# First stage of a gated cross-attention layer: x loaded from ScalarE's queue, weights alone in SyncE's and rounded one unit ahead, context and two units of weights loaded ahead of x

## What is computed

```python
x = x + tanh(g_xattn[0]) * xattn(layernorm(x), ctx, ctx, mask, wq, wk, wv, wo)
x = x + tanh(g_ffn[0]) * ffn(layernorm(x), weight, bias, gate_w, in_scale, out_scale)

# xattn: 32 query heads, 8 heads of keys and values, 128 wide, rotary positions
q = rope(heads(layernorm(x) @ wq)); k = rope(heads(ctx @ wk)); v = heads(ctx @ wv)
out = softmax(q @ k.T / sqrt(128) + mask) @ v;  return merge(out) @ wo
```

## Time and profile before

| | us |
|---|---|
| median of 3 runs (1532.45 to 1533.03) | 1532.85 |
| the profiled execution, its own time | 1532.2 |
| its span, first to last instruction | 1530.4 |
| PE busy in the span | 1485.5 (97%) |
| POOL busy | 723.7 (47%) |
| ACT busy | 613.2 (40%) |
| DVE busy | 1032.1 (67%) |
| share of PE in the chain that ended last | 83% |
| first matmul of the second stage starts at | 90.57 |

### The profile page before, as it was taken

How to read it: one execution, slowest core, us unless ns; L and a number is a source line. 1 busy time by engine, 2 the same in 40 slices (tenths; PEclk the granted TensorE clock), 3 DMA queues, 4 the chain that set the end, 5 groups by cost and what they waited for, 6 DMA issues and landing times.

```text
span 1530.4 us, 26067 instructions
## 1 busy us (share of the span) xinstructions
PE 1485.5 (97%) x8720; PEld 1307.6 (85%) x8720; DVE 1032.1 (67%) x2373; ACT 613.2 (40%) x1183; POOL 723.7 (47%) x594
## 2 busy tenths in 40 slices
PE   5989999999999999999999989999999999989998
PEld 5868888888888888888888879999999999977886
DVE  5837888888877888888887784455455555765653
ACT  5732222222222212222222255555567555634442
POOL 6834445654555445554465453333333333335554
PEclk9999999999999999999999999999999999999999
DMA  7830222212221322212221596443997443542311
GB/s 272 287 110 27 71 76 69 69 48 69 75 69 45 85 69 75 69 41 75 69 69 44 166 361 227 132 131 100 369 390 230 134 125 102 185 141 109 110 74 64
DMA packets 95210, 192.56 MB, mean 126 GB/s; under 512 B 9056, under 2 KB 36192, under 8 KB 95008
## 3 DMA queue, kind: packets, MB, share of 16 engines
q1 hardware_dynamic: 88944, 179.74, 36.4%
q10 hardware_dynamic: 6192, 11.86, 2.3%
HBM read 133.90 MB, written 57.67 MB: 125 GB/s over the span
## 4 chain that ended last, share of the span: by engine, by line
PE 83%; DMA 3%; issue 3%; POOL 2%; DVE 1%; SPq 1%; ACT 1%; POOLq 0%; ACTq 0%; DVEq 0%
PE bank L54 19%; PE bank L53 19%; PE bank L52 19%; PE bank L916 7%; PE bank L915 7%; PE bank L914 7%; PE bank L937 5%; DMA w_raw<-in_wo 2%; POOL last_rows L1352 1%; PE bank L950 1%; DVE project L1504 1%; SPq L689 0%; POOL feed L1344 0%; ACT project L1130 0%; DMA signs_scratch<-rows 0%
## 5 line engine op out<-in xcount | busy, mean ns | idle before, releaser
L52 PE MATMUL bank<-x_hi,w_hi 128*128 128x512 f32 x1024 | 399.6, 390 | 3.9 <-PEq L67 3.9
L54 PE MATMUL bank<-x_hi,w_lo 128*128 128x512 f32 x1024 | 400.6, 391 | 0.0
L53 PE MATMUL bank<-x_lo,w_hi 128*128 128x512 f32 x1024 | 400.0, 391 | 0.0
L1504 DVE TENSOR_TENSOR project<-bank,project 64x256 fp32r<-64x256 f32 x512 | 216.1, 422 | 196.0 <-ACT project L1130 190.6
L1357 POOL TENSOR_TENSOR w_lo<-w_raw,w_hi 128x512 fp32r<-128x512 f32 x128 | 166.4, 1301 | 283.8 <-ACT w_hi L1122 283.8
L1291 POOL TENSOR_TENSOR q_lo<-rot,q_hi 128x512 fp32r<-128x512 f32 x128 | 165.0, 1295 | 188.4 <-ACT q_hi L1061 188.2
L1130 ACT CAST project<-bank 64x256 fp32r<-64x256 f32 x512 | 187.6, 366 | 159.2 <-PE bank L54 150.4
L915 PE MATMUL bank<-project,project 128*128 128x256 f32 x832 | 236.3, 284 | 0.0
L914 PE MATMUL bank<-project,project 128*128 128x256 f32 x832 | 236.2, 284 | 0.0
L916 PE MATMUL bank<-project,project 128*128 128x256 f32 x832 | 235.9, 284 | 0.0
L52 PEld LDWEIGHTS bank<-x_hi,w_hi 128*128 128x128 f32 x1024 | 192.7, 188 | 45.4 <-issue 4.1
(11 more groups left out here) (143 smaller groups left out, 2683.8 us busy)
## 6 DMA issues: line engine op xcount, KB each, us to landing
w_raw<-in_wo SPq DMA_DIRECT2D x128, 256.0 KB, 3.0
project<-probs_scratch SPq DMA_DIRECT2D x52, 512.0 KB, 8.8
w_raw<-in_wq SPq DMA_DIRECT2D x32, 512.0 KB, 5.2
probs_scratch<-pt_hi SPq DMA_DIRECT2D x64, 256.0 KB, 2.6
probs_scratch<-pt_lo SPq DMA_DIRECT2D x64, 256.0 KB, 3.2
x_in<-in_x SPq DMA_DIRECT2D x16, 512.0 KB, 5.0
last_rows<-in_x SPq DMA_DIRECT2D x8, 1024.0 KB, 6.1
x_scratch<-last_rows SPq DMA_DIRECT2D x8, 1024.0 KB, 6.0
```

The costliest lines, as they stand in the source:

```text
L52: pe.matmul(out, hi, rhs_hi, start=first, stop=False, **kw)
L53: pe.matmul(out, hi, rhs_lo, start=False, stop=False, **kw)
L54: return pe.matmul(out, lo, rhs_hi, start=False, stop=last, **kw)
L1504: done = nc.vector.tensor_tensor(vw_lo[i][at], vw_ps[hp % VW_BANKS][b * SK:(b + 1) * SK, h, :], vw_hi[i][at].bitcast(F32), ALU.subtract)
```

## The change

Five edits, all in `prepare`:

1. On SP, both halves of the context and units 0 and 1 are issued first, then blocks 0 to 2 of x. From then on SP loads only weights, and it takes over the stores of keys and values, at fixed places between the loads (`KEYS_AT`, `VALUES_AT`), with the waits at the end of the stage.
2. On ACT, `load_x(n + 3)` stands in iteration n right behind `normalise(n)`, whose result it waits for.
3. On ACT, `split_unit` runs one unit ahead: unit 0 between the two halves of the context, and unit n + 1 at the head of iteration n, ahead of `normalise(n)`.
4. On POOL, `reciprocal_deviation(0)` no longer stands ahead of the loop; iteration n makes `w_lo` of unit n and then `reciprocal_deviation(n - 1)`.
5. On DVE, the low part of the context comes ahead of the statistics of block 0.

```diff
@@ SyncE
+    KEYS_AT, VALUES_AT = 6, HKV + 6
-            def load_x(i):
-                wait(sp, xn_ready, i - XB + 1)
-                sp.dma_start(x_in[:, i % XB], a["x"][i * P:(i + 1) * P, :]).then_inc(x_in_sem[i % XB], 16)
+            def store_keys(gp):
+                sp.wait_ge(k_roped, gp + 1)
+                for c in range(2):
+                    sp.dma_start(scratch["keys"][c, gp * P:(gp + 1) * P, :], k_rot[:, 2 * c, :]).then_inc(k_stored, 16)
+
+            def store_values(g):
+                sp.wait_ge(v_lo_ready, g + 1)
+                for c, part in enumerate((v_hi, v_lo)):
+                    sp.dma_start(scratch["values"][c, g], part[:, g % 2].bitcast(F32)).then_inc(v_stored[g % 2], 16)
 
             for h in range(2):
                 src = a["ctx_t"].rearrange("(k p) t -> p k t", p=P)[:, half(h)]
                 sp.dma_start(ctx_raw[:, half(h)], src).then_inc(ctx_in[h], 16)
-                if h == 0:
-                    load_unit(0)
-                    load_x(0)
-            load_unit(1)
-            load_x(1)
-            load_x(2)
+                load_unit(h)
+            for i in range(XB):
+                sp.dma_start(x_in[:, i], a["x"][i * P:(i + 1) * P, :]).then_inc(x_in_sem[i], 16)
             for n in range(2, UNITS):
                 load_unit(n)
-                if n + 1 < NLN:
-                    load_x(n + 1)
+                if n >= KEYS_AT and n % 2 == 0 and (n - KEYS_AT) // 2 < GP:
+                    store_keys((n - KEYS_AT) // 2)
+                if n >= VALUES_AT:
+                    store_values(n - VALUES_AT)
+            for g in range(UNITS - VALUES_AT, HKV):
+                store_values(g)
...
@@ ScalarE
+            def load_x(i):
+                act.wait_ge(xn_ready, i - XB + 1)
+                act.dma_start(x_in[:, i % XB], a["x"][i * P:(i + 1) * P, :]).then_inc(x_in_sem[i % XB], 16)
...
             for h in range(2):
                 act.wait_ge(ctx_in[h], 16)
                 nc.scalar.copy(ctx_hi[:, half(h)], ctx_raw[:, half(h)]).then_inc(ctx_hi_ready, 1)
+                if h == 0:
+                    split_unit(0)
             for n in range(NU + 2):
-                split_unit(n)
+                if n + 1 < UNITS:
+                    split_unit(n + 1)
                 if n < NLN:
                     normalise(n)
+                if n + XB < NLN:
+                    load_x(n + XB)
                 if HKV <= n - 1 < NU:
                     value_high(n - 1 - HKV)
                 if n >= 2:
                     turned(n - 2)
-
-                if 0 <= n - 2 < HKV and (n - 2) % 2 == 1:
-                    store_keys((n - 2) // 2)
-                if n - 2 >= HKV:
-                    store_values(n - 2 - HKV)
...
@@ GpSimd
-            reciprocal_deviation(0)
             for n in range(UNITS):
                 for h in range(2):
                     pool.wait_ge(w_hi_ready, 2 * n + h + 1)
 
                     nc.gpsimd.tensor_tensor(w_lo[:, n % 2, half(h)], raw(n)[:, half(h)], w_hi[:, n % 2, half(h)].bitcast(F32),
                                             ALU.subtract).then_inc(w_lo_ready, 1)
-                if n + 1 < NLN:
-                    reciprocal_deviation(n + 1)
+                if 0 <= n - 1 < NLN:
+                    reciprocal_deviation(n - 1)
@@ VectorE
-            statistics(0)
             for h in range(2):
                 dve.wait_ge(ctx_hi_ready, h + 1)
                 ...
+            statistics(0)
```

More of the change, by code:

```diff
@@ L149, in _ @@
                 sp.dma_start(ctx_raw[:, half(h)], src).then_inc(ctx_in[h], 16)
-                if h == 0:
-                    load_unit(0)
-                    load_x(0)
-            load_unit(1)
-            load_x(1)
-            load_x(2)
+                load_unit(h)
+            for i in range(XB):
+                sp.dma_start(x_in[:, i], a["x"][i * P:(i + 1) * P, :]).then_inc(x_in_sem[i], 16)
             for n in range(2, UNITS):
                 load_unit(n)
-                if n + 1 < NLN:
-                    load_x(n + 1)
+                if n >= KEYS_AT and n % 2 == 0 and (n - KEYS_AT) // 2 < GP:
[4 more added lines that the diff above has]
+                store_values(g)
+            sp.wait_ge(k_stored, 32 * GP)
+            for i in range(2):
+                sp.wait_ge(v_stored[i], 32 * HKV // 2)
         @block.tensor
@@ L215, in turned @@
                 last.then_inc(x_hi_ready, 1)
[L217 to L225, removed]
             act.dma_start(ident[:], a["ident"]).then_inc(ident_in, 16)
@@ L240, in _ @@
                     turned(n - 2)
-                if 0 <= n - 2 < HKV and (n - 2) % 2 == 1:
-                    store_keys((n - 2) // 2)
-                if n - 2 >= HKV:
-                    store_values(n - 2 - HKV)
-            act.wait_ge(k_stored, 32 * GP)
-            for i in range(2):
-                act.wait_ge(v_stored[i], 32 * HKV // 2)
         @block.gpsimd
```

## The result

| | before | changed |
|---|---|---|
| median of 6 runs, us | 1532.94 (1531.31 to 1535.17) | 1568.83 (1566.58 to 1570.67) |
| ratio | 1 | 1.0236, 95% interval 1.0224 to 1.0247 |
| span of the profiled execution | 1530.4 | 1565.6 |
| first matmul of the second stage | 90.57 | 126.33 |
| block 0 normalised at | 12.82 | 14.79 |

The change makes the kernel 2.4% slower, and all of it lies ahead of the barrier: from the first matmul of the second stage to the end it is 1530.4 - 90.57 = 1439.8 us before and 1565.6 - 126.33 = 1439.3 after.

What follows compares the result with a forecast made beforehand. It took a first-stage cycle across ACT, POOL and PE as the bound, lengthened from 4.14 to 6.86 us a unit. Start, iterations and tail put the second stage 35.3 us later: 1532.2 + 35.3, plus 0.65 for the median, 1568.0; range 1558 to 1577.

Steps and rivals of the forecast that it cites:

- Terms 1 and 2: First-stage cycle: start of `w_hi` to start of `w_lo`, 0.71 us; from there to the normalisation behind it, 3.61.
- Term 3: On ACT, normalisation to first cast of `x_hi`, with the load issue now between them: 1.60 us instead of 1.15.
- Term 4: On ACT, from the casts of `x_hi` to the next `w_hi`: 0.94 us.
- The cycles: Time per first-stage unit: 6.86 us in key units instead of 4.14, 7.12 in value units, 6.67 without a load.
- The beginning: Start of the first stage: context and units land before x, so block 0 is normalised at 15.6, not 12.82.
- The sum up to block 15: First-stage iterations added from 15.6: block 15 normalised at 117.2 against 79.32, 37.9 us later.
- The tail: From block 15's normalisation through casts, `x_lo` and half-clock transposes to the second stage's first matmul at 125.8, against 90.57.
- the rival of the half clock: TensorE at half clock paces the first stage at 7.2 us a unit: 1573; chance 0.12 together with a dearer issue.
- Stores on SP, nothing: Moving the stores of keys and values to SP's queue costs no time; loads there have cycles in hand.
- the ring: First stage: ACT's split, POOL's `w_lo`, then `shift`, then ACT's normalisation run one after another, 6.86 us a unit.
- the hidden issue: Rival: ACT's casts start 1.15 us after the normalisation despite the load issue, 5.9 us less, 1562; chance 0.13.
- The faster rival: Normalisation does not wait for the next unit's `w_lo`; cycle is PE's 3.9 us, kernel 1522; chance 0.04.

Runs made afterwards that it cites:

- the one POOL edit: Changed kernel with POOL's small operations of block n right behind the low part of unit n, not of unit n + 1; 1525.7 us, ratio 0.9958.
- the version with the values on SP: Units a cycle sooner (all loads on SP, block n of x behind unit n), with only the stores of values moved from ACT's queue to SP's; 1523.63 us.
- the kernel with the new beginning alone: Kernel before, with context and units 0 and 1 loaded ahead of x and DVE's statistics of block 0 behind the context; 1534.93 us, ratio 1.0015.

## Why the prediction was right

1568.0 was forecast, 1568.83 measured, against 1532.94. The steps, one by one:

- *The stage is a piece in front with a barrier behind it.* Right, by the 1439.8 and 1439.3 above. That the two agree to 0.5 us is partly luck: over all profiled executions this part took 1439.2 to 1444.4 us with no edit in it. So the total, forecast to 0.8 us, is nearer than such a sum can promise; the cycles are the better test.
- *Terms 1 and 2*, 0.71 and 3.61 (sum 4.32). Measured 0.71 and 3.59.
- *Term 3*, the load issue, 1.60. Measured 1.65: 0.04 between the end of the issue and the cast was left out. The Trainium skill (Perfetto Trace Analysis, Per-instruction lifecycle) has a DMA's wait hold the sequencer, and the trace agrees: the cast at 35.70, ready long before, started behind the issue that ended at 35.66. With the loads on SP the same distance is 1.14 and the kernel 7.5 us faster.
- *Term 4*, 0.94. Measured 0.96.
- *The cycles.* 6.86 forecast and 6.91 measured for key units (27.16 to 75.56 in seven), 7.12 and 7.21 for value units with a load, 6.67 and 6.65 without.
- *The beginning.* 15.6 forecast, 14.79 measured. This step was mis-sized, and its reading was wrong. I took the 2.46 us of the first three small operations for a cost of being first. They took 1.13 here (13.66 to 14.79), though they were as much the first; the next section says why. In the other direction the `w_lo` ahead of them took 3.02 instead of 2.52.
- *The sum up to block 15.* 117.2 forecast, 117.70 measured: 0.8 too much at the start, 0.5 too little in the first two iterations (one of which took 3.96 from `w_lo` to the normalisation, because the two engines held each other up as the last section describes), 0.8 too little for the 0.05 to 0.09 of each of the 11 cycles with a load.
- *The tail.* 8.6 forecast, 8.63 measured, with transposes of 1.94 us at half clock. Two small slips stand in the last sums: 125.8 - 90.57 is 35.2 and not 35.3, and 1532.2 + 35.2 + 0.65 is 1568.1 and not 1568.0. In the rival of the half clock, 13.7 - 2.4 - 5.1 is 6.2 and not 6.1. None of them changes a conclusion.
- *Stores on SP, nothing.* SP waited 31.7 us for rotated keys and 31.9 for values, and nobody waited for SP. The four waits for keys were 7.9 us on average, more than the one cycle after which the prediction had the results complete, and SP was still ahead, as it held for that case. The cover is no property of the slow cycle: with the ring open and the stores placed as in the change, SP waited 22.0 us for keys and 11.2 for values (the one POOL edit), and ACT did not wait for weights after the beginning. It was lost where the loads of x stood in SP's queue too: 16.2 us of ACT's time, and still 9.2 with the stores of keys back at their place.

Of the rivals, the hidden issue is excluded by term 3. The half clock came as its row suggested it might, in part of the iterations, and cost the cycles nothing: with PE at half clock from 59.00 to 64.8, ACT's normalisations stood at 61.70 and 68.62, 6.92 apart. In the tail it is on the path, and the sum had counted it there. The prediction read from the earlier trace rows that waits of about 1 us leave the full clock; the waits of those iterations were only 0.2 to 0.6 us, but in the changed kernel a wait of 1.42 us (before 24.61) did leave it. The Trainium skill (TensorE: Matmul & The Clock Gate, Part 1) has the low level as the default; by the means of 0.78 to 0.91 the stage was not at the low level throughout. The faster rival was put at a cycle of 3.9 and 1522; that about this much was kept from the kernel by the ring is shown by the POOL edit (1525.7), and cycles of 3.89 a unit were reached with the loads on SP (1523.6).

## What to carry to other kernels

When work on one engine is moved ahead of other work, write down for each engine what now stands in front of what, and follow the dependences across engines: a partner engine whose order was moved as well, as here, can turn two streams that ran beside each other into one, and the sign of it is two waits that name each other, once per iteration. A queue's order has to be moved along with the order of its consumer. A load behind an instruction that waits for the newest result is late as soon as the consumer runs one step ahead, and each such wait hides the next: here three were taken away one after another for 1533.1, 1528.0, 1527.6 and 1523.6 us. The version that left the waiting loads of x on a queue of their own had a first stage as short without any of this (82.94, 82.67 and 81.50 us, against 82.96).

## What the runs showed of the hardware that was not expected

VectorE and GpSimd hold each other up when VectorE runs an operation that reads two inputs from SBUF (the on-chip memory in which all tiles but those of PSUM lie) while GpSimd reads there too, and the profile shows this as busy time, not as a wait. The rotation's last two operations (two inputs in SBUF) take 0.42 us each in the kernel before. In the changed kernel the first pair fell on POOL's `w_lo`; DVE's rows and POOL's:

```profile
23.47 1.27 DVE L299 TENSOR_TENSOR k_rot<-k_rot 128x256 f32<-128x256 f32 x1
24.67 1.52 DVE L300 TENSOR_TENSOR k_rot<-k_rot 128x256 f32<-128x256 f32 x1
```
```profile
23.20 2.70 POOL L271 TENSOR_TENSOR w_lo<-ctx_raw,w_hi 128x512 fp32r<-128x512 f32 x2 [2.44 <-ACT w_hi L208]
25.86 0.73 POOL L258 TENSOR_TENSOR rstd<-var_eps,minus_half 128x1 f32<-128x1 f32 x1
```

The later pairs, which fell between two `w_lo`, took 0.43 and 0.42 again. The operations next to them that read one input from PSUM took at most 0.43 in the first stage of every trace, and the statistics, with a single input in SBUF, took 1.29 beside POOL's `w_lo` as elsewhere. In the version with the one POOL edit such a collision lies on the path, since POOL's next small operations wait for the statistics that stand behind the rotation on DVE. DVE's rows, then those of POOL and the ACT row that waits for them:

```profile
31.93 1.53 DVE L299 TENSOR_TENSOR k_rot<-k_rot 128x256 f32<-128x256 f32 x1
33.38 1.48 DVE L300 TENSOR_TENSOR k_rot<-k_rot 128x256 f32<-128x256 f32 x1
```
```profile
31.88 2.71 POOL L271 TENSOR_TENSOR w_lo<-ctx_raw,w_hi 128x512 fp32r<-128x512 f32 x2
37.77 0.55 POOL L258 TENSOR_TENSOR rstd<-var_eps,minus_half 128x1 f32<-128x1 f32 x1 [3.18 <-DVE var_eps L287]
38.89 1.24 ACT L218 ACTIVATE xn<-x_in,shift,rstd 128x1024 f32<-128x1024 f32 x1 [2.92 <-POOL shift L262]
```

The normalisation before that one stands at 32.20, so this cycle took 6.69 us where its neighbours took some 3.7 to 4.1. It is so in all three executions of this version (6.68 and 6.73 in the others). In the version with the values on SP the same two operations took 0.42 each, and the cycle there 3.93. So the version with the one POOL edit, 7 us faster than the kernel before, still loses some 2 us to the collision. That is an estimate from these rows (3.0 us for the two operations instead of 0.8); no run took it out alone.

This is also what had looked like a cost of being first. In the kernel before, the 1.40 us of the earlier trace rows at 10.36 ran beside the low part of the context on DVE (10.12 to 12.47); in the kernel with the new beginning alone, the same first operation ran without it:

```profile
13.03 0.56 POOL L254 TENSOR_TENSOR rstd<-var_eps,minus_half 128x1 f32<-128x1 f32 x1 [12.14 <-DVE var_eps L284]
```

The Trainium skill (SBUF — State Buffer, SBUF: two separate sides) has the two engines share a pair of ports, held by one instruction for its whole length, with a VectorE operation with two SBUF inputs among those that need it; the rows above agree. No run took this collision alone out of the changed kernel, so its share of the 36 us that the change costs is only read from rows: 3.96 instead of 3.59 in one iteration, and 0.5 in the `w_lo` of unit 1.
